# A decoder layer of 32 sequences: queries and outputs of cross attention turned dense and placed by DMA, recurrent squares in three of four blocks

## What is computed

```python
# recurrent attention, per chunk of 64 steps
att = rr @ kk * Wm          # Wm: w**(t-s-1) below the diagonal, u on it, 0 above
y = att @ vv + rr @ state * wb
state = ws * state + kk * wkv @ vv
...
y = (zn * ln_g + ln_b) * g  # zn: y normalised per head, g = silu
return y @ Wo.T + bo
# cross attention
scores = jnp.einsum('bkgsd,bktd->bkgst', qh, kh) / scale
out = jnp.einsum('bkgst,bktd->bkgsd', softmax(scores), vh)
# feed forward
h = mx_linear(mx_gelu(mx_linear(mx_layernorm(x), W1, b1)), W2, b2)
```

## Time and profile before

| | |
|---|---|
| time, median of 3 runs | 1406.24 us (1405.39 to 1407.93) |
| profiled execution, its own time | 1410.62 us |
| its span in the profile | 1408.8 us |
| TensorE busy | 93% of the span |
| VectorE busy | 87% |
| ScalarE busy | 63% |
| GpSimd busy | 40% |
| granted TensorE clock, mean | 0.966 |
| DMA | 62.60 MB, 18.9% of the 16 engines' span on the program's queue |

### The profile page before, as it was taken

The page is one execution under the profiler, slowest core; times in us unless marked ns, Lnnn a source line. Parts: engine busy times, 40 slices in busy tenths (PEclk is TensorE's granted clock), DMA queues, the critical chain, the costliest instruction groups (busy, mean ns, idle before and its releaser), DMA issues.

```text
span 1408.8 us, 30713 instructions
## 1 busy us (share of the span) xinstructions
PE 1304.6 (93%) x11592; PEld 843.2 (60%) x11592; DVE 1228.0 (87%) x2026; ACT 889.8 (63%) x1763; POOL 563.3 (40%) x608
## 2 busy tenths in 40 slices
PE   2788999999999999999999999999999999999854
PEld 2665666666666666666566666655666666655421
DVE  6898988889899989899899999988999998888675
ACT  2345575766766676766666676766667677666541
POOL 4554444433334444333334444333334444332232
PEclk8789999999999999999999999999999999999877
DMA  9243201111111011211211011111111011111112
GB/s 306 69 102 95 57 13 26 37 37 38 37 28 37 16 33 38 37 37 37 37 28 30 22 34 37 37 37 37 37 28 29 20 37 37 37 36 31 20 35 49
DMA packets 149858, 62.60 MB, mean 44 GB/s; under 512 B 137040, under 2 KB 138064, under 8 KB 148944
## 3 DMA queue, kind: packets, MB, share of 16 engines
q1 hardware_dynamic: 149712, 60.63, 18.9%
HBM read 26.53 MB, written 8.39 MB: 25 GB/s over the span
## 4 chain that ended last, share of the span: by engine, by line
PE 66%; DVE 12%; issue 12%; DMA 5%; POOL 2%; ACT 2%; SPq 0%; POOLq 0%; DVEq 0%; ACTq 0%
PE bank_b L417 14%; PE bank_a L417 6%; PE bank_y L521 6%; PE bank_y L456 5%; PE bank_a L407 5%; PE rt L477 4%; PE rt L490 4%; PE bank_y L442 4%; PE rt L429 3%; PE bank_o L496 3%; PE bank_b L512 3%; PE bank_a L512 2%; PE bank_o L450 2%; DMA gmem<-w 2%; DMA out<-x 2%
## 5 line engine op out<-in xcount | busy, mean ns | idle before, releaser
L3065 POOL TENSOR_TENSOR x<-x,o_bf 128x512 f32<-128x512 f32 x32 | 37.1, 1160 | 448.4 <-DVE o_bf L1565 448.4
L2458 ACT ACTIVATE pT<-rt 128x2048 f32<-128x2048 f32 x64 | 119.6, 1869 | 70.0 <-PE rt L490 67.5
L1418 DVE TENSOR_TENSOR att<-rt,wm 128x2048 f32<-128x2048 f32 x64 | 146.5, 2289 | 15.0 <-PE rt L429 14.9
L3060 POOL TENSOR_TENSOR gmem<-gmem,unit_g 128x1024 bf16<-128x1024 bf16 x64 | 124.1, 1939 | 60.2 <-DVE unit_g L1498 60.2
L1447 DVE TENSOR_REDUCE negm<-rt 128x16 f32<-128x2048 f32 x64 | 146.4, 2287 | 1.6 <-PE rt L477 1.3
L521 PE MATMUL bank_y<-w2q,gmem 128*128 128x512 bf16 x512 | 121.6, 392 | 19.3 <-DMA gmem<-gmem 19.3
L417 PE MATMUL bank_b<-mix_k,w_Wk 128*128 128x128 f32 x1024 | 127.5, 286 | 12.8 <-DVE mix_k L1395 12.8
L417 PEld LDWEIGHTS bank_b<-mix_k,w_Wk 128*128 128x128 f32 x1024 | 125.5, 203 | 14.7 <-issue 12.5
L417 PE MATMUL bank_a<-mix_r,w_Wr 128*128 128x128 f32 x1024 | 125.2, 282 | 4.2 <-POOL mix_r L3031 4.2
L417 PEld LDWEIGHTS bank_a<-mix_r,w_Wr 128*128 128x128 f32 x1024 | 119.1, 195 | 8.4 <-POOL mix_r L3031 4.6
L417 PE MATMUL bank_b<-mix_g,w_Wg 128*128 128x128 f32 x1024 | 121.7, 278 | 0.0
(11 more groups left out here) (193 smaller groups left out, 2867.1 us busy)
## 6 DMA issues: line engine op xcount, KB each, us to landing
xin<-x SPq DMA_DIRECT2D x32, 256.0 KB, 2.7
gmem<-w SPq DMA_DIRECT2D x16, 512.0 KB, 4.1
out<-x SPq DMA_DIRECT2D x32, 256.0 KB, 2.0
kv<-ctx SPq DMA_DIRECT2D x32, 64.0 KB, 2.7
pT<-Wv SPq DMA_DIRECT2D x1, 1024.0 KB, 10.1
b1row<-b SPq DMA_DIRECT2D x1, 1024.0 KB, 12.1
w_Wg<-Wg SPq DMA_DIRECT2D x1, 1024.0 KB, 14.5
w_Wo<-Wo SPq DMA_DIRECT2D x1, 1024.0 KB, 16.4
```

The costliest lines, as they stand in the source:

```text
L1418: e.tensor_tensor(att[:, :, :, :, :].rearrange("p g m a t -> p (g m a t)"), rt[:, :], wm[:, i, :, :, :, :].rearrange("p g m a t -> p (g m ...
L2458: e.activation(pT[:, :, :].rearrange("p g n -> p (g n)"), rt[:, :], ACT.Exp, scale=float(D) ** -0.5).then_inc(sem(f"act_ex{i}"), 1)
L3060: e.tensor_tensor(blocks(half), blocks(half), per_block(unit[f"g{i}"], 32), ALU.mult).then_inc(sem(f"pool_gsc{i}"), 1)
```

## The change

Recurrent part: the three quarters of a square that are not zero are made as three blocks of 64 columns. `receptance` writes r once (4 operations); GpSimd makes the odd/even pairs, of the later half of r (`later_receptances`) and of the earlier half of k (`earlier_keys`). `scores_r` becomes 16 matmuls a half in place of 8: 8 of 128 columns and 8 of 64. `decayed` runs over 1536 columns in place of 2048. Values: `vz` keeps the heads by parity with zeros between, two DMAs (`earlier_values`) copy its first 64 rows into `vp` with the odd heads in the lower 64 rows, and `values_r` becomes 24 matmuls of 64 columns a half in place of 16 of 128.

Cross attention: the host pads the context, adds the ones and also turns it, and one load brings both forms (256 KB a sequence in place of 64 KB). Queries are written dense and turned by 4 transposes in place of 10; 8 DMAs (`queries_spread`) put them at their padded rows. Outputs are gathered by 8 DMAs and the sums of weights by 2 (`outputs_gathered`), turned by 4 transposes in place of 8 plus one small one for the sums (`turn_sums`), and divided by one reciprocal and one multiplication in place of two each.

All queues are put in a new order; the stages that one step works on stay the same ones. The core of the diff:

```diff
             def load_ctx(n):
...
+                e.dma_start(both[n % 2][:, :], ctx_in[n]).then_inc(sem(f"sp_ctx{n % 2}"), 16)
+
+            def earlier_values(n):
+                e.wait_ge(sem("dve_vz"), n + 1)
...
+                for a in range(2):
+                    e.dma_start(vp[HALF * a:HALF * a + HALF, :, :].rearrange("p q c -> p (q c)"),
+                                vz[0:HALF, a * H * D:(a + 1) * H * D]).then_inc(sem("sp_vp"), 16)
+
+            def queries_spread(n, i):
+                e.wait_ge(sem("act_qdense"), n + 1)
...
+                for g in range(4):
+                    kvh = 4 * i + g
+                    e.dma_start(qx[32 * g:32 * g + D, i, :, :], qdense[D * kvh:D * kvh + D, :, :]).then_inc(sem(f"sp_qx{i}"), 16)
+
+            def outputs_gathered(n, i):
+                e.wait_ge(sem(f"act_oT{i}"), n + 1)
...
+                e.dma_start(oden[D * i:D * i + D, :], oT[D:P:32, i, :, :].rearrange("g j t -> g (j t)")).then_inc(sem("sp_oden"), 16)
+                for g in range(4):
+                    kvh = 4 * i + g
+                    e.dma_start(odense[D * kvh:D * kvh + D, :, :], oT[32 * g:32 * g + D, i, :, :]).then_inc(sem("sp_odense"), 16)
...
+            for n in range(10, 29):
+                store(n - 6)
+                queries_spread(n - 3, 0)
+                maxima_to_rows(n - 3)
+                load_ctx(n - 2)
+                hidden_turned(n - 4)
+                gelu_turned(n - 5, 0)
+                outputs_gathered(n - 3, 0)
+                gelu_turned(n - 5, 1)
                 next_x(n)
+                earlier_values(n - 1)
+                outputs_gathered(n - 3, 1)
+                queries_spread(n - 2, 1)
...
             def scores_r(n, i):
...
+                e.wait_ge(sem("pool_kz"), n + 1)
+                e.wait_ge(sem("pool_rz"), n + 1)
...
+                        e.matmul(rtb(g)[:, mm * 3 * HALF:(mm * 3 + 2) * HALF], kT[rows32, m, :], rz[rows32, m, :, :],
+                                 start=True, stop=True)
...
+                        done = e.matmul(rtb(g)[:, (mm * 3 + 2) * HALF:(mm * 3 + 3) * HALF], kz[rows32, m, :, :],
+                                        rT[rows32, m, 0:HALF], start=True, stop=True)
...
             def values_r(n, i):
...
+                    e.wait_ge(sem("sp_vp"), 32 * (n + 1))
...
+                        done = e.matmul(bank_y[32 * g:32 * g + 32, m * T:m * T + HALF], vp[:, 4 * m + g, :],
+                                        att[:, g, mm, 2, :], start=True, stop=True)
...
+                            done = e.matmul(bank_y[32 * g:32 * g + 32, m * T + HALF:(m + 1) * T], vz[:, at:at + 2 * D],
                                             att[:, g, mm, a, :], start=(a == 0), stop=(a == 1))
...
+            def turn_queries(n):
+                e.wait_ge(sem("act_xq"), n + 1)
+                for j in range(GQ):
+                    done = e.transpose(rtb(0)[:, j * T:(j + 1) * T], xq[:, j, :], ident[:, :])
+                done.then_inc(sem("pe_XT"), 1)
+
+            def scores_max(n, i):
                 e.wait_ge(sem(f"sp_ctx{n % 2}"), 16 * (n // 2 + 1))
...
+                e.wait_ge(sem(f"sp_qx{i}"), 64 * (n + 1))
...
+            def turn_sums(n):
+                e.wait_ge(sem("sp_oden"), 32 * (n + 1))
+                e.transpose(bank_o[:, 0:H], oden[:, :], ident[0:H, 0:H]).then_inc(sem("pe_dT"), 1)
+
+            def turn_out(n):
+                e.wait_ge(sem("sp_odense"), 128 * (n + 1))
                 for j in range(GQ):
...
+                    done = e.transpose(bank_o[:, j * P:(j + 1) * P], odense[:, j, :], ident[:, :])
+                done.then_inc(sem("pe_ot"), 1)
...
+            for n in range(10, 29):
+                e.wait_ge(sem("dve_rd"), n - 3)
+                turn_x(n - 1)
+                e.wait_ge(sem("dve_o"), n - 5)
+                values_r(n - 2, 0)
+                e.wait_ge(sem("act_xT"), n)
+                turn_out(n - 4)
+                e.wait_ge(sem("act_qdense"), n - 2)
+                scores_max(n - 3, 1)
...
+                project("g", n - 2, bank_b, "pool")
...
+                scores_max(n - 3, 0)
...
+                project("r", n - 1, bank_a, "pool")
...
+                scores_r(n - 2, 1)
...
+                turn_maxima(n - 3)
...
+                project("k", n - 1, bank_b, "dve")
+                values_r(n - 2, 1)
...
+                scores_x(n - 3, 0)
...
+                head_variance(n - 2)
...
+                project_v(n - 1)
...
+                values_x(n - 3, 0)
...
+                scores_x(n - 3, 1)
...
+                up(n - 4, 1, bank_b)
...
+                up(n - 4, 0, bank_a)
...
+                project_out(n - 2)
                 e.wait_ge(sem("act_oT0"), n - 2)
                 values_x(n - 3, 1)
...
+                scores_r(n - 1, 0)
...
+                down(n - 5, 0)
+                down(n - 5, 1)
                 e.wait_ge(sem("dve_Ra0"), n)
+                turn_queries(n - 2)
                 e.wait_ge(sem("act_oT1"), n - 2)
+                turn_sums(n - 3)
...
+                up(n - 4, 2, bank_a)
                 e.wait_ge(sem("dve_ze1"), n - 3)
                 up(n - 4, 3, bank_b)
...
+                e.tensor_tensor(att[:, :, :, :, :].rearrange("p g m k t -> p g (m k t)"),
+                                rt[:, :].rearrange("p (g n) -> p g n", g=4)[:, :, 0:6 * HALF],
+                                wm[:, i, :, :, :, :].rearrange("p g m k t -> p g (m k t)"), ALU.mult).then_inc(sem(f"dve_Ra{i}"), 1)
...
                 for m in range(KT):
...
+                    done = e.activation(rT[:, m, :], bank_a[:, m * T:(m + 1) * T], ACT.Identity,
+                                        bias=col["br"][:, m:m + 1])
+                done.then_inc(sem("act_rT"), 1)
...
+            def of_parity(n, name, out, src, after):
...
+                e.tensor_tensor(out[:, :, :, :], src.unsqueeze(2).to_broadcast([P, KT, 2, HALF]),
+                                parity.unsqueeze(1).unsqueeze(3).to_broadcast([P, KT, 2, HALF]),
+                                ALU.mult).then_inc(sem(name), 1)
...
+                mixed(n - 1, "r")
+                second_sum(n - 4)
+                with_bias(n - 2)
+                mixed(n - 1, "g")
+                gate_parts(n - 2)
+                later_receptances(n - 1)
+                gate_rstd(n - 2)
+                earlier_keys(n - 1)
+                gelu_scale(n - 5, 1)
+                gelu_scale(n - 4, 0)
+                last_sum(n - 5)
```

More of the change, by code:

```diff
@@ L286, in _ @@
             next_x(5)
+            outputs_gathered(2, 1)
+            earlier_values(4)
+            queries_spread(3, 1)
+            store(0)
+            queries_spread(3, 0)
+            maxima_to_rows(3)
+            gelu_turned(1, 0)
             load_ctx(4)
-            store(0)
-            maxima_to_rows(3)
             hidden_turned(2)
-            gelu_turned(1, 0)
             gelu_turned(1, 1)
+            outputs_gathered(3, 0)
             next_x(6)
+            earlier_values(5)
@@ L294, in _ @@
+            outputs_gathered(3, 1)
+            queries_spread(4, 1)
             store(1)
-            load_ctx(5)
+            gelu_turned(2, 0)
+            queries_spread(4, 0)
             maxima_to_rows(4)
             hidden_turned(3)
-            gelu_turned(2, 0)
+            load_ctx(5)
             gelu_turned(2, 1)
+            outputs_gathered(4, 0)
             next_x(7)
+            earlier_values(6)
+            outputs_gathered(4, 1)
+            queries_spread(5, 1)
+            store(2)
@@ L354, in _ @@
             gelu_turned(27, 0)
+            outputs_gathered(29, 0)
+            load_ctx(30)
             gelu_turned(27, 1)
-            load_ctx(30)
-            load_ctx(31)
+            earlier_values(31)
+            outputs_gathered(29, 1)
+            queries_spread(30, 1)
+            queries_spread(30, 0)
             store(27)
@@ new lines, in _ @@
+            gelu_max(5, 0)
+            gelu_pow2(5, 0)
+            decayed(8, 0)
+            stats_q(9)
+            norm_mv("q", 9)
+            second_out(4)
+            residual(4)
+            gelu_round(5, 0)
+            for n in range(10, 29):
+                denominators(n - 4)
+                differences(n - 1)
+                up_out(n - 5, 3, bank_b)
+                up_out(n - 5, 2, bank_a)
+                normalise_o(n - 4)
+                maxima(n - 3, 1)
+                stats_f(n - 4)
+                norm_mv("f", n - 4)
+                maxima(n - 3, 0)
+                mixed(n - 1, "k")
+                gate(n - 2)
+                gelu_quantised(n - 5, 0)
+                decayed(n - 2, 1)
+                stats_g(n - 4)
+                norm_mv("g", n - 4)
+                mixed(n - 1, "v")
+                weighted(n - 4)
+                hidden(n - 4)
+                hidden_max(n - 4)
+                hidden_pow2(n - 4)
+                hidden_scale(n - 4)
+                hidden_round(n - 4)
+                hidden_quantised(n - 4)
```

(26 more changed lines are left out.)

2062 lines of the change are left out of this document (913 added, 1149 removed).

## The result

| | before | after |
|---|---|---|
| median of the runs, us | 1406.84 (1405.39 to 1407.93) | 1428.53 (1427.9 to 1435.24) |
| profiled execution / its span, us | 1410.6 / 1408.8 | 1427.9 / 1426.1 |
| the eighth `turn_x` begins at | 307.4 | 314.4 |
| 24 steps, eighth to last `turn_x` | 954.7 (39.78 each) | 958.7 (39.95 each) |
| an undisturbed step | 39.4 | 39.0 |

The ratio is 1.0166 [1.0134, 1.0198]: slower, where 1373.5 was forecast. Of the 17.3 us between the two spans 7.0 lie in the first sequences, 4.0 in the 24 steps and 6.3 at the end. No part got shorter.

The account below looks back on a forecast made before the run. TensorE's list was taken as the bound, VectorE 3.4 us behind. A step: -1.57 + 0.20 + 0.15 = -1.22, over 26 steps -31.7; first six -5, end +4: -32.7 from the median 1406.24 gives 1373.5, range 1344 to 1408.

Parts of the forecast that it names:

- TensorE's list: TensorE's matmul groups in a loop step: context and queries 0.80, outputs 0.25, `values_r` 0.47, `scores_r` 0.05 saved, together 1.57.
- that rival: Narrow bundles are not cheaper: `values_r` loses 0.74, `scores_r` saves nothing; 1406, no change; chance 0.10.
- Each microsecond that leaves TensorE's list shortens a step, until VectorE takes over: Loop step of 39.40 us: TensorE busy throughout, no wait on its chain; VectorE takes over 3.4 us behind.
- ScalarE is not on the chain: ScalarE, at 27.7 of 39.4, loses copies: no gain in the sum, except that `queries_x` finds it free.
- The wait at `scores_max`: TensorE waits there for `queries_spread`: 4.2 against 4.1 of cover, so 0.1, taken as 0.2 a step.
- the middle rival's price: SyncE's issues cost 0.59, not 0.35, and the stall at `scores_max` is 0.9: 1393; chance 0.16.
- the 0.2 for hops between engines: Allowance in the queries' round trip ahead of `scores_max`, raising 3.97 to 4.2.
- the landing of the earlier trace: A small DMA lands 1.89 after its issue began; used for the queries' copies ahead of `scores_max`.
- my allowance for stalls: TensorE stalls from VectorE, held by GpSimd's new operations: 0.15 a step (0 to 0.6).
- the first six sequences: Steps bound by VectorE: -1.46 + 0.6 = -0.86 each, -5 in all.
- The end: Drain of the last sequences: new round trips in a row once or twice, +4 (0 to 10).
- The slower rival: SyncE's order makes the queries land 2.4 us after TensorE wants them: +0.98 a step, 1432; chance 0.14.

Follow-up runs that it names:

- the run of 1450: Changed kernel with queries turned as before, normalise_q ahead of the queries' copies on ScalarE, decayed and x's statistics ahead of gelu_max on VectorE: 1450.05 (1.0294).

## Why the prediction was wrong

**TensorE's list: right in kind, 0.45 too large.** Forecast -1.57 a step; read from start to start in both kernels it is -1.12: queries 1.15 to 0.53 (-0.62, forecast -0.80), outputs 0.94 to 0.77 (-0.17, but the g projection behind them takes 0.11 more; forecast -0.25), `values_r` 2.00 to 1.62 (-0.38, forecast -0.47), `scores_r` 2.16 to 2.10 (-0.06, forecast -0.05). The chain of the earlier trace rows gives a group its time up to its modelled end, which overlaps the next group's start (by 0.06 us at 680.79 in the timeline of after), so I subtracted more than the group had cost; and what a group takes beyond 0.109 a transpose is as much for four as for eight: 0.53 for 0.44 here, 0.97 for 0.87 with the queries undone (705.67 to 706.64). The total can be tested: the kernel with the queries undone and no wait should take 39.4 less 0.28 (context), 0.38, 0.06 and 0.06, 38.62; its steps are 38.65. That it fits to 0.03 is in part luck: the eight transposes take 0.97 there, so the context saves 0.18, `values_x` takes 0.11 more, and `down`, `up` and the turned maxima take 0.17 less. The narrow bundles are cheaper, 0.81 a half for 0.99 and 1.01, so that rival falls.

**"Each microsecond that leaves TensorE's list shortens a step, until VectorE takes over": this is the step that failed first.** TensorE was full, but two rings (chains of waits that go through several engines and back to TensorE) were as long to within tenths of a microsecond. In the kernel before it is store, `normalise_o`, `turn_x`: the context's part alone takes 0.22 from the list and gives nothing, and a third buffer alone, which takes the store out of the ring, gives 4 us. The earlier trace rows had it: `normalise_o` idle for 17.5 us behind the store. I used that row for a duration alone. In after it is the queries' turning, ScalarE's copy, `normalise_q`, `turn_x`: 0.42 in every step, of which I had counted none. I wrote that ScalarE is not on the chain; I didn't ask what stands behind `queries_x` on it while it waits for a turning that now comes later. One line moved there is worth 15 us (1412 to 1397).

**The wait at `scores_max`: right for a good step, wrong for 7 of the 24.** The issues of the queries' four copies are 0.55 to 0.64 apart (75 of 81 from sequence 5 on), not 0.35: the middle rival's price, an assumption I had taken from x, a load from memory, against the only on-chip copy in the earlier trace rows. In a good step the wait is still 0.1 to 0.2, as forecast, but, by the order of the queue, only since TensorE loses 0.42 at `turn_x` first; no run has the copies without that loss. The mean is 0.64 (0.70 with two waits for VectorE's maxima) through the late landings, 1.3 to 2.0 each. Of the 0.2 for hops between engines, a guess in the sum, the trace of after shows 0.13 from the landing to TensorE's start and 0.03 from ScalarE's end to the first issue. I had taken the landing of the earlier trace rows as a constant. By size this is the larger failure: without the round trip the kernel takes 1398, 31 of the 55 us between forecast and result.

**The clock.** Four of the waits over 1 us at `scores_max` in the 24 steps are followed, within 2.1 us, by stretches at a granted clock of 0.50, half the full one (the longest from 517.53 to 524.36), 17 us together; the longest step of 43.8 has 6.8 of them and its g projection takes 6.4 in place of 3.8:

```profile
517.13 1.77 PE L596 MATMUL rt<-context,qx 16*128 16x128 f32 x32 [1.67 <-DMA qx<-qdense]
518.84 6.35 PE L530 MATMUL bank_b<-mix_g,w_Wg 128*128 128x128 f32 x31
```

Other waits as long are not followed by one, and what tells them apart is open. The kernel without the queries' copies has no half clock in its 24 steps, nor has the kernel before; three without that round trip have some, 3.4 to 6.8 us, each beside a wait of 1.35 or more at `turn_x` (the context's part alone, context and recurrent squares, and the run of 1450). The seven steps with a late landing are 17.1 us above 39.0 together, clock included: as much as the forecast's 1.22 a step gives in 14 steps.

**The steps added up.** Forecast 39.78 - 1.22 = 38.56, measured 39.95, 1.39 more: 0.45 list, 0.42 `turn_x`, 17.1 / 24 = 0.71 late landings, 0.23 other stalls, less 0.38 of the stalls of before that went and 0.05 where my allowance for stalls was above what a good step has. Over 24 steps that is 33 of the missed 50 us between the spans.

**Start and end.** Forecast -5 for the first six sequences, measured +7.0 at the eighth `turn_x`. Without the copies it is +0.2: the round trips cost 7, and the lighter VectorE gives nothing. Between 50 and 100 us it is busy for 41.55 where it was 45.79; it waits more. In the start of the kernel with context and recurrent squares one such wait on GpSimd could be named; which wait of after costs how much there was not taken apart. The end: +4 forecast (0 to 10), +6.3 measured, 3.6 of it the copies.

**The slower rival** gave 1432, near the result, by another mechanism. SyncE was through with `outputs_gathered` a microsecond before the queries were ready (753.46 against 754.54), so its order set nothing there. That its time came near is luck. I gave it 0.14 and left it out of the range; what was missing was a bound for the landing and a look at the rings, not SyncE's queue.

## What to carry to other kernels

A full engine is not the only bound: before counting a gain in its list, find for every wait in that list the ring that feeds it and how much slack it has, because the first tenths taken from the list may all go there. A round trip by DMA in a tight place needs its slack against the late landing (here 3.2 to 4.0 us from issue to TensorE's start), not the median (2.1), and its length in issues of the same kind of copy. When a step adds a wait on an in-order queue, write down everything behind it on that engine; moving one independent operation ahead was worth 15 us here, more than context and recurrent squares together (1403 to 1395).

## What the runs showed of the hardware

- The 108 packets of the instruction queue in after are of 16 KB each and take 0.88 to 1.72 us, 1.09 in the median; TensorE has 256 records for each. In all 21 late sequences from the fifth on, of after and the two kernels with more transposes, one of them began 1.0 to 1.9 us after the last of four 32 KB copies was issued. In the two sequences read mark by mark, one part in sixteen of that copy landed 1.3 and 1.7 us behind the other fifteen (397.14 and 398.44 in after; 748.22 and 749.92 with the store moved). With some 10 packets in three steps, 6 to 8 of 27 sequences had a late landing.
- A 32 KB copy between on-chip buffers took 0.55 to 0.64 us to issue in 75 of 81 cases, and from the issue of the fourth to TensorE's start passed 2.07 to 2.14 us in the 20 of 27 sequences of after without a late landing.
- Four 64-column matmuls on different column groups took little over half of four with 128: six such bundles in 0.36 us (678.12 to 678.48 above), 0.06 each, against 0.109. A half of `values_r`, 48 records, takes 0.81, 17 ns for each.
